# A smaller first routing batch, ranked earlier and in another PSUM bank, and the token scatter moved forward by three tiles

## The reference

```
x = x + spikes(relu(attn0(x) @ Wfc.T)**2 @ Wproj.T)
X = attn1(x)                                # 16 heads, one key and value head
X = X + block_attention(rmsnorm(X))         # 4 heads
xf = rmsnorm(X)
rw = softmax(xf @ Wr.T + expert_bias)       # 8 experts
topw, topi = top_k(rw, 2); topw = softmax(topw)
specialist = sum over the two chosen e of topw[e] * swiglu(xf, eW1[e], eW2[e], eW3[e])
x = x + X + swiglu(xf, sW1, sW2, sW3) + specialist
```

## Time and profile before

| | |
|---|---|
| time, median of 3 runs | 1470.36 us (1470.21 to 1470.57) |
| the profiled execution, own time | 1471.9 us |
| its span, first to last instruction | 1470.1 us |
| mean granted TensorE clock | 0.950 |
| busy: PE, DVE, ACT, POOL | 89%, 70%, 61%, 50% |
| 64 sends, L885 | 64.6 us busy, 1126.3 to 1231.4 us |
| block's last 12 steps (30 to 41) | 1072.8 to 1130.5 us |
| 72 routed tiles on TensorE | from 1235.8 us |

### The profile page before, as it was taken

How to read it: one execution, slowest core, us unless ns; L and a number is a source line. 1 busy time by engine, 2 the same in 40 slices (tenths; PEclk the granted TensorE clock), 3 DMA queues, 4 the chain that set the end, 5 groups by cost and what they waited for, 6 DMA issues and landing times.

```text
span 1470.1 us, 43158 instructions
## 1 busy us (share of the span) xinstructions
PE 1308.9 (89%) x15310; PEld 1158.7 (79%) x15311; DVE 1035.6 (70%) x2136; ACT 899.7 (61%) x2312; POOL 729.2 (50%) x829
## 2 busy tenths in 40 slices
PE   4899999998699999799999998789987788999980
PEld 3799999997589999688888886578876677888870
DVE  4798888888645646787787877688875765555545
ACT  4677777676366667466667665477864343555545
POOL 2555565645244545455544444588844563333330
PEclk9899999999799999999999999899988799999995
DMA  8200000001030000000000001100012523333319
GB/s 226 53 9 9 8 10 8 10 8 38 1 85 1 1 0 1 5 9 9 9 9 8 9 9 29 47 17 14 13 34 76 192 81 97 100 103 101 102 46 343
DMA packets 87016, 71.06 MB, mean 48 GB/s; under 512 B 49982, under 2 KB 80832, under 8 KB 85825
## 3 DMA queue, kind: packets, MB, share of 16 engines
q1 hardware_dynamic: 80320, 51.73, 12.3%
q0 software_dynamic: 6528, 17.05, 3.2%
HBM read 39.47 MB, written 24.02 MB: 43 GB/s over the span
## 4 chain that ended last, share of the span: by engine, by line
PE 58%; issue 20%; POOL 11%; DVE 4%; ACT 3%; DMA 2%; another core or an unknown queue 0%; SPq 0%; DVEq 0%; ACTq 0%; POOLq 0%
PE psQ L2327 9%; PE psQ L1937 7%; PE psW L2015 7%; PE psW L2306 5%; POOL pn L754 4%; PE psQ L2128 3%; PE psS L2128 3%; PE psW L2116 3%; PE psM L2116 3%; POOL rq L780 3%; PE psT L1966 2%; PE psS L2039 2%; PE psT L2050 2%; PE psM L1989 2%; PE psT L2295 2%
## 5 line engine op out<-in xcount | busy, mean ns | idle before, releaser
L1937 PE MATMUL psQ<-xT,wq 128*128 128x256 f32 x1536 | 224.9, 298 | 3.3 <-ACT cur L1103 1.8
L1937 PEld LDWEIGHTS psQ<-xT,wq 128*128 128x128 f32 x1536 | 204.9, 201 | 4.4 <-issue 2.5
L2015 PE MATMUL psW<-wout,oT 128*128 128x256 f32 x1536 | 203.4, 290 | 1.1 <-ACT oT L966 1.1
L2015 PEld LDWEIGHTS psW<-wout,oT 128*128 128x128 f32 x1536 | 192.3, 195 | 1.3 <-ACT oT L966 1.3
L2327 PE MATMUL psQ<-W,exT 128*128 (+1 forms) x624 | 175.4, 418 | 0.0
L754 POOL TENSOR_TENSOR pn<-ex,rden 128x1024 f32<-128x1024 f32 x64 | 124.5, 1946 | 43.8 <-DVE rden L1429 43.8
L798 POOL TENSOR_TENSOR hT<-hf,hT 128x512 fp32r<-128x512 f32 x64 | 85.8, 1341 | 103.1 <-ACT hT L1099 102.9
L966 ACT ACTIVATE oT<-psT,small 128x512 fp32r<-128x512 f32 x128 | 81.1, 684 | 90.2 <-PE psT L2050 90.2
L901 POOL DMA_INDIRECT results<-result,idx x72 | 70.1, 974 | 132.5 <-ACT result L1231 129.1
L766 POOL TENSOR_TENSOR masked_bias<-bias_t,negmask 128x1024 f32<-128x1024 f32 x32 | 68.8, 2150 | 132.5 <-DVE ex L1397 132.5
L2327 PEld LDWEIGHTS psQ<-W,exT 128*128 128x128 f32 x624 | 113.1, 195 | 19.1
(11 more groups left out here) (298 smaller groups left out, 3416.1 us busy)
## 6 DMA issues: line engine op xcount, KB each, us to landing
rows<-sorted SPq DMA_DIRECT2D x72, 132.0 KB, 2.1
both<-results SPq DMA_DIRECT2D x8, 1024.0 KB, 12.7
raw_w<-W SPq DMA_DIRECT2D x27, 256.0 KB, 3.7
vv<-vp SPq DMA_DIRECT2D x256, 16.0 KB, 1.8
out<-X SPq DMA_DIRECT2D x8, 512.0 KB, 9.8
X<-x SPq DMA_DIRECT2D x1, 3584.0 KB, 17.9
bvv<-v_all SPq DMA_DIRECT2D x128, 16.0 KB, 1.8
sorted<-rows SPq DMA_DIRECT2D x9, 132.0 KB
```

What stands on the lines that cost most here:

```text
L1937: mm = nc.tensor.matmul(psQ[:, cc, h * QT:h * QT + QT], wq[w][:, k, c * P:c * P + P], xT[g % 2][u][:, k, :], start=(k == 0 and j == 0), st ...
L2015: mm = nc.tensor.matmul(psW[:, 0:D], oT[u][:, c, :], wout[w][:, c, :], start=(u == 0 and c == 0 and w == 0), stop=(u == 1 and c == CH - 1))
```

## The change

Four things, all in the order of work and none in what is computed:

- Batch 0 has 20 tiles and batch 1 has 12 (before 24 and 8).
- Batch 0's parts move three expert steps earlier: BELOW, FIRST_CHOICE, SECOND_CHOICE, RANK and PLACES at s = -6, -5, -4, -2 and -1, that is after block steps 30, 31, 32, 34 and 35. Batch 1's stay. `first_half` is therefore called from i = 28 on.
- Batch 0 is ranked in `psT[:, 0, :]`, the bank that holds the block's transposed queries, once ScalarE has taken the last of them (`t_kT`); batch 1 still in `psM`.
- GpSimd's sends go through `send_tile`. Tiles 0, 1 and 2 are sent after GpSimd's block steps 36, 37 and 38 without waiting for `e_xTp`; tile t from 3 on waits for `e_xTp` of t-2, three tiles less than before.

```diff
--- before.py
+++ after.py
@@ -57,8 +57,9 @@
 MERGE = TILES + 4
 BEHIND = 10
 BEGUN = TILES + BEHIND - MERGE
-BATCHES = ((0, 3 * TILES // 4), (3 * TILES // 4, TILES))
-BELOW, FIRST_CHOICE, SECOND_CHOICE, RANK, PLACES = (-3, 5), (-2, 6), (-1, 7), (1, 8), (2, 9)
+BATCHES = ((0, 20), (20, TILES))
+BELOW, FIRST_CHOICE, SECOND_CHOICE, RANK, PLACES = (-6, 5), (-5, 6), (-4, 7), (-2, 8), (-1, 9)
+SENT_AHEAD = 3
 ENDS, SLOTS, TOP_WEIGHTS = 10, 11, 12
 NOWHERE = 1 << 20
 BUFS = 8
@@ -501,10 +502,15 @@
 
             return psS[:, 1, 0:E] if isinstance(i, int) and i >= MERGE else psW[:, D:D + E]
 
+        def rank_columns(b):
+
+            n = BATCHES[b][1] - BATCHES[b][0]
+            return (psM[:] if b else psT[:, 0, :])[:, 0:(n + 1) * E]
+
         def rank_bank(b):
 
             n = BATCHES[b][1] - BATCHES[b][0]
-            v = psM[:, 0:(n + 1) * E].rearrange("p (t e) -> p t e", e=E)
+            v = rank_columns(b).rearrange("p (t e) -> p t e", e=E)
             return v[:, 0:n, :], v[:, n, :]
 
         def swapped(v):
@@ -878,7 +884,8 @@
                         nc.gpsimd.iota(what[:], pattern=[[step, n]], base=0, channel_multiplier=0,
                                        allow_small_or_imprecise_dtypes=True).then_inc(sem("const_pool"), 1)
 
-            pipeline(pool, block_step, 1, 4, 10, numbers)
+                elif 0 <= i - TILES - 4 < SENT_AHEAD:
+                    send_tile(i - TILES - 4)
 
             def send(t, k):
 
@@ -886,13 +893,20 @@
                                              in_=xf_all[:, t, :], in_offset=None, bounds_check=UNUSED - 1,
                                              oob_is_err=False).then_inc(sem("x_sent"), 16)
 
-            for b, (low, high) in enumerate(BATCHES):
-                pool.wait_ge(sem("r_placed"), b + 1)
-                pool.wait_ge(sem("d_xfa"), high)
-                for t in range(low, high):
-                    pool.wait_ge(sem("e_xTp"), t + 1)
-                    for k in range(TOP_K):
-                        send(t, k)
+            def send_tile(t):
+
+                for b, (low, high) in enumerate(BATCHES):
+                    if t == low:
+                        pool.wait_ge(sem("r_placed"), b + 1)
+                        pool.wait_ge(sem("d_xfa"), high)
+                if t >= SENT_AHEAD:
+                    pool.wait_ge(sem("e_xTp"), t - SENT_AHEAD + 1)
+                for k in range(TOP_K):
+                    send(t, k)
+
+            pipeline(pool, block_step, 1, 4, 10, numbers)
+            for t in range(SENT_AHEAD, TILES):
+                send_tile(t)
 
             def store_result(r, m):
 
@@ -1251,7 +1265,7 @@
             def merged(i):
                 if i >= MERGE:
                     expert_step(i - MERGE, (i - MERGE) % BUFS, kind(i - MERGE, None))
-                if i >= TILES:
+                if i >= TILES - 4:
                     first_half(i - MERGE)
 
             pipeline(act, block_step, 1, 4, BEHIND, merged)
@@ -2339,8 +2353,11 @@
 
                 low, high = BATCHES[b]
                 n = high - low
-                bank = psM[:, 0:(n + 1) * E].rearrange("p (t e) -> p t e", e=E)
-                pe.wait_ge(sem("t_olo"), 2 * BLK + TILES)
+                bank = rank_columns(b).rearrange("p (t e) -> p t e", e=E)
+                if b == 0:
+                    pe.wait_ge(sem("t_kT"), BLK + TILES)
+                else:
+                    pe.wait_ge(sem("t_olo"), 2 * BLK + TILES)
                 pe.wait_ge(sem("r_given"), b + 2)
                 nc.tensor.matmul(bank, before[:], chosen[:, low:high + 1, :], start=True, stop=False, skip_group_check=True)
                 for t in range(n):
```

## The result

The changed kernel takes 1455.64 us (median of 4 runs, 1451.01 to 1458.99), the kernel before 1470.46 us beside it (1470.21 to 1471.44). The ratio is 0.9902, with a 95% interval of 0.9873 to 0.9931: 14.8 us faster.

What follows compares the result with a forecast made beforehand. TensorE was taken to bound the routed tiles, with GpSimd's last sends and the block-end ring limiting before them. Terms -7.3 - 0.3 + 0.3 = -7.3 us took 1470.36 to 1463.1 us, range 1457.5 to 1470.0.

Steps and rivals of the forecast that it cites:

- Part 1: Before the first routed tile: TensorE's wait for sorted rows goes and its first step runs at full clock, -7.3 us.
- Rival B: At the scatter's end: GpSimd's own pace eats the lead, the wait stays, gain 2 to 3 us; chance 0.10.
- Part 2: GpSimd's six early sends in the block's last steps: they delay its block work under cover, cost 0.
- step 39: Block's end: PLACES leaves VectorE, where TensorE waited 1.01 us for `xf`; -1.0 us, bounds 0 and 1.0.
- Part 3: Batch 0's routing pieces put into block steps 30 to 32 add 5.5 us, bounds 4.5 and 8.9.
- The fourth term: TensorE idles in the gaps, so its clock falls some steps earlier: +1.0 us, bounds 0 and 2.
- step 35: Block's end: FIRST_CHOICE gone, RANK in TensorE's gap behind step 34; -2.0 us, bounds 1.0 and 2.75.
- Part 4: Routing pieces leaving or replaced in block steps 33 to 39 give back 5.8 us, bounds 2.0 and 8.1.
- Part 5: Batch 1 with 12 tiles: about 30 VectorE operations grow slightly, +0.3 us, bounds 0 and 0.9.
- Rival C: A TensorE stall during SP's expert weight loads changes by 4 us; chance 0.08 for worse, 0.06 for better.
- Rival A: Block steps 31 to 34: the ring pays more than the wait returns, slower at 1473.9 us; chance 0.08.
- The sign named for it: Last logits of the block later than 1134, listed as showing parts 3 and 4 wrong.

Runs made afterwards that it cites:

- before_again: The kernel before, unchanged, measured against itself on a chip without standstills: 1449.48 us, ratio 0.9995.
- after_third: The changed kernel, unchanged, on a chip without standstills: 1437.51 us, ratio 0.9910 to the kernel before.
- rank_late_again: rank_late repeated on the chip of rank_fill: 1448.35 us, ratio 0.9981 to the kernel before.
- rank_late: Changed kernel with tiles 0 to 2 sent after the block steps and batch 0's RANK and PLACES at their old steps and bank: 1448.99 us, ratio 0.9984.
- rank_fill: rank_late with 21 small matmuls, read by nobody, added on TensorE behind block step 34: 1445.88 us, ratio 0.9969 to the kernel before.
- after_again: The changed kernel once more, unchanged, on the chip where the kernel before takes 1469.89 us: 1457.48 us, ratio 0.9919.
- after_split: Changed kernel with the last part of SP's expert weight loads held until shared tile 12 is transposed: 1439.42 us, ratio 0.9916 to the kernel before.

## Why the prediction was wrong in size

**Part 1, the scatter's end: right here, the number partly by luck.** -7.3 predicted, -7.26 measured, with no wait and a first step of 2.55 us at full clock. The last send came earlier than the 1221 to 1223 given, because TensorE's own end of the shared tiles did; the cover is 1.6 us and not 2.6. On a chip without standstills the same term is -8.6 (before_again and after_third), so -7.3 is the figure of a chip with them. One reason was too good: that GpSimd "isn't behind there" was read from one wait for TensorE on a chip with standstills. Rival B (GpSimd's own pace keeps the wait) is true of the lead alone on both chips without them that ran it; only with the early placements, another part of the same change, does it fail.

**Part 2, the early sends: right on the cost, 0.** VectorE's `xf` of step 38 waits for ScalarE (1.90 us) and that of step 39 for nothing, so GpSimd's add and root behind the sends are done in time. Beyond the first, which takes 1.23 us before and after, the early sends take 0.98 to 1.03 us where 0.98 is usual. But they also bring nothing.

**Part 3, the added pieces: right but for the clock.** Step 31 grew by 0.63 us (predicted 1.0), step 32 by 2.69 (2.6), step 33 by 1.24 (0.9): 4.56 us, where the three terms were 4.5. The fourth term, "its clock, which is at 0.50 by 1098, will fall some steps earlier", priced at +1.0, is one that failed. The clock did fall earlier (0.83 and 0.92 in steps 32 and 33, where it was 1.00), but at little cost: step 32 takes 6.86 us at 0.83 and 6.44 at 1.00 (rank_late_again). And it did not stay down: it was 1.00 in step 35, where it had been 0.50.

**Part 4, what goes: the step that failed is step 35.** Predicted -2.0, with bounds of 1.0 and 2.75; measured -3.74. The text knew that RANK would lie in TensorE's gap and counted it only as work, 1.6 us in a gap of 1.49. It bounded the gain by 2.75 us, the time that VectorE was late, as though TensorE's own 1.62 us for the projection were fixed. As work alone the term was right: in rank_late and rank_late_again, without RANK behind step 34, step 35 is 1.88 and 2.57 us shorter than before. The other 1.2 to 1.9 us are the clock that matmuls in the gap hold: rank_fill, with matmuls that nobody reads in RANK's place, has step 35 at 3.99 us as the changed kernel.

A second term of part 4 was mis-sized, and not by the clock: step 39, predicted -1.0 with 1.0 as its bound, measured -2.04. The bound was the 1.01 us that TensorE waited for an `xf`. But VectorE itself was busy without a break; timeline of VectorE in that step before, its first and last rows and the first and last of the placements (2.21 us in all):

```profile
1122.48 0.42 DVE L1846 TENSOR_TENSOR eh<-sg,psQ 128x256 f32<-128x256 f32 x1 [1.17 <-ACT sg L1220]
...
1123.15 0.35 DVE L1796 TENSOR_TENSOR place_of<-psM,next_row 128x192 f32<-128x192 f32 x1
...
1125.20 0.16 DVE L1802 TENSOR_TENSOR next_row<-psM,next_row 128x8 f32<-128x8 f32 x1
...
1126.26 0.16 DVE L1677 TENSOR_TENSOR logits<-psS,ebias 128x8 f32<-128x8 f32 x1
```

So nearly all of the placements came off the step. rank_fill, whose clock is 1.00 there as well and whose placements stay, has 4.93 us for it; the changed kernel has 3.07.

The other steps: 34 -0.94 (-0.8), 36 -0.38 (-0.2), 37 +0.38 (0), 38 -2.08 (-1.8). The net of parts 3 and 4 was -4.2 us where -0.3 stood, and beyond the low bound of -3.6. Of these 3.9 us, step 35 is 1.7, step 39 1.0 and the clock's +1.0 that hardly came 0.9.

**Part 5** (+0.3): T5 to T9, T9 to T24 and T24 to T31 on a chip without standstills are 13.9, 45.9 and 17.8 us after, 13.4, 46.0 and 17.8 before; +0.4.

**Rival C, a stall elsewhere changes, came true for the better** in the first trace, beside the forecast: T5 to T31 went from 97.2 to 92.4 us. after_again, with 96.1, speaks for chance; its median, 12.4 us below before, is nearer to what the two other terms give. The case stood by itself with 0.06, and its 4 us were not added to the others in the range. The three terms, -7.3, -4.2 and -4.8, are 16.3 of the 16.9 us between the profiled spans; the medians differ by 14.8. On a chip without standstills the two systematic terms alone give -12.7 (before_again and after_third), with medians 13.8 us apart; after_split, on another, is 11.8 us below before.

**Rival A** needed the block's end 10 us later. The logits of step 39 were 4.5 us earlier. The sign named for it, last logits later than 1134, did come (1134.43), but from the standstills in step 41: without them steps 40 and 41 take 1.78 and 3.05 us (after_third).

## What to carry to other kernels

In a ring where engines hand one tile round, look at the granted clock of each step before pricing an edit: a move of small matmuls into TensorE's gaps is worth not what they cost but what the clock gives to the steps after them, and if no useful ones are to be had, matmuls that nobody reads do it as well (shown here in the steps' lengths; the medians did not resolve it). Bound what a removed piece gives back by the busiest engine of that step, not by the wait of another. A lead in a queue must be built up somewhere: check that the slower producer has spare time between its first possible start and the point where the lead is wanted. And read a margin that rests on one engine's wait on a trace without standstills, if there is one.

## What the runs showed that was not expected

- 21 small bf16 matmuls of no use (1.03 us on TensorE) shortened the four steps behind them by 4.1 to 5.3 us.
- The same kernel takes 1469.9 us on one chip and 1451.2 to 1451.7 on four others. The difference lies in standstills of all engines (20 us between T5 and T31 in the traces of before: 97.2 against 77.1), with VectorE and ScalarE busy for the same time (1035.6 and 899.7 us against 1035.3 and 900.2) and TensorE for 8 us less (1308.9 against 1300.9). The logits of step 30, before which no kernel changed anything, scatter over 6 us from trace to trace.
- A standstill can show on an engine's row as a wait for another engine (6.33 us "DVE ehT" above), while the rows that end it on the others name no engine (6.70 us "remote" on ScalarE): the rows that name none tell that it was a standstill, though not what caused it.
